# Value evictions to ScalarE with their bias as rows of the product, and row maxima placed anew

## The reference, cut to what matters

```python
x = x + attn0(layernorm(x)); x = x + experts(...); x = x + bit_mlp(...)
x = x + attn1(layernorm(x)); x = x + xattn(layernorm(x), ctx, mask); x = x + fp8_linear(...)

# each attention
q, k, v = (a @ W.T + bias for ...)          # v: 512 x 512 a sequence, bias along the features
probs = softmax(q @ k.T * 32 ** -0.5)       # for each of 16 heads (cross: clipped and masked)
out = concat_heads(probs @ v) @ Wo.T + bo
```

## Time and profile before

| | us |
|---|---|
| median of 3 runs | 1939.64 |
| lowest, highest | 1937.99, 1941.87 |
| the profiled execution | 1936.93 |
| its span | 1935.1 |
| TensorE busy | 1572.5 |
| VectorE busy | 1209.4 |
| ScalarE busy | 835.3 |
| POOL busy | 486.6 |

### The profile page before, as it was taken

The page is one execution under the profiler, slowest core; times in us unless marked ns, Lnnn a source line. Parts: engine busy times, 40 slices in busy tenths (PEclk is TensorE's granted clock), DMA queues, the critical chain, the costliest instruction groups (busy, mean ns, idle before and its releaser), DMA issues.

```text
span 1935.1 us, 28229 instructions
## 1 busy us (share of the span) xinstructions
PE 1572.5 (81%) x9252; PEld 608.8 (31%) x9253; DVE 1209.4 (62%) x1767; ACT 835.3 (43%) x991; POOL 486.6 (25%) x408
## 2 busy tenths in 40 slices
PE   2899899998948953777689999999959989989827
PEld 1323223232236631343332323233223333323213
DVE  3754747647545636999665464646544676767678
ACT  1252352533523323777635344353634445453622
POOL 1513216033120014311121212212123231414125
PEclk9999999999969986988899999999979999999968
DMA  3700202002024445100030110202222020203002
GB/s 116 238 16 22 65 0 69 18 22 65 26 105 140 138 103 114 22 1 0 11 100 10 32 34 6 60 0 65 87 72 60 22 65 22 65 1 86 0 28 87
DMA packets 80843, 106.08 MB, mean 55 GB/s; under 512 B 14112, under 2 KB 51360, under 8 KB 80672
## 3 DMA queue, kind: packets, MB, share of 16 engines
q1 hardware_dynamic: 77216, 97.14, 17.0%
q0 software_dynamic: 3584, 8.39, 2.1%
HBM read 49.26 MB, written 18.35 MB: 35 GB/s over the span
## 4 chain that ended last, share of the span: by engine, by line
PE 45%; issue 22%; DVE 18%; POOL 7%; ACT 3%; DMA 2%; DVEq 1%; POOLq 0%; ACTq 0%; SPq 0%
PE ps L398 18%; PE ps L713 13%; PE ps L799 6%; PE ps L663 3%; DVE arena L909 2%; DVE xn L186 2%; POOL arena L1117 2%; POOL arena L1177 2%; PE ps L685 1%; DVE arena L1603 1%; PE ps L1490 1%; DVE stats L175 1%; ACT arena L888 1%; DVE arena L1076 1%; POOL rstd L199 1%
## 5 line engine op out<-in xcount | busy, mean ns | idle before, releaser
L888 ACT ACTIVATE arena<-ps 128x1024 f32<-128x1024 f32 x384 | 374.0, 1023 | 346.4 <-PE ps L799 345.2
L713 PE MATMUL ps<-arena 128*32 128x512 f32 x3072 | 399.1, 625 | 33.7 <-DVE arena L943 24.4
L909 DVE TENSOR_REDUCE arena<-ps 128x2 f32<-128x1024 f32 x256 | 306.8, 1220 | 162.9 <-PE ps L663 162.9
L398 PE MATMUL ps<-xt,w 128*128 128x512 f16 (+1 forms) x1872 | 301.0, 313 | 32.4 <-DVE arena L977 20.4
L799 PE MATMUL ps<-arena 97*128 97x512 f16 (+1 forms) x768 | 221.7, 402 | 16.5 <-DVE arena L992 14.4
L398 PEld LDWEIGHTS ps<-xt,w 128*128 128x128 f16 (+1 forms) x1872 | 155.8, 101 | 169.1 <-issue 66.5
L398 PE MATMUL ps<-w,arena 128*128 128x512 f16 (+1 forms) x804 | 178.7, 379 | 12.7 <-issue 12.7
L1177 POOL TENSOR_TENSOR arena<-arena 128x512 f16<-128x512 f32 x96 | 114.9, 1199 | 239.0 <-ACT arena L877 203.4
L873 ACT ACTIVATE arena<-ps,arena 128x512 f32<-128x512 f32 x96 | 65.7, 685 | 226.0 <-PE ps L398 190.0
L1093 POOL TENSOR_TENSOR arena<-arena 128x512 f32<-128x512 f32 x36 | 50.3, 1398 | 421.7 <-DVE arena L948 421.7
L1076 DVE TENSOR_SCALAR arena<-arena 128x1024 f32<-128x1024 f32 x128 | 106.7, 839 | 65.3 <-ACT arena L888 64.8
(11 more groups left out here) (169 smaller groups left out, 1849.1 us busy)
## 6 DMA issues: line engine op xcount, KB each, us to landing
arena<-arena SPq DMA_DIRECT2D x576, 64.0 KB, 2.0
raw<-in_ctxT SPq DMA_DIRECT2D x8, 1024.0 KB, 5.4
raw<-in_ffn_parts SPq DMA_DIRECT2D x16, 512.0 KB, 3.6
sorted_x<-arena SPq DMA_DIRECT2D x1, 4864.0 KB, 27.1
arena<-sorted_x SPq DMA_DIRECT2D x19, 256.0 KB, 3.5
sorted_y<-arena SPq DMA_DIRECT2D x19, 256.0 KB, 2.1
out<-x SPq DMA_DIRECT2D x16, 256.0 KB, 2.1
x<-in_x SPq DMA_DIRECT2D x1, 3072.0 KB, 14.3
```

The source lines that it names most:

```text
L398: last = pe.matmul(out, left[l](cl[k]), right[r](cr[k]), start=start and k == 0 and a == 0, stop=stop and k == n - 1 and a == 2)
L713: last = pe.matmul(self.m.ps[HD * j:HD * (j + 1), 7 if ones else 6, :], left, self.pt[:, u % 2, j * S:(j + 1) * S], start=kb == 0, stop=kb ...
L888: act.activation(self.pt[:, u % 2, 2 * h * S:(2 * h + 2) * S], flat(self.m.ps[:, 2 * h:2 * h + 2, :]), ACT.Exp, scale=SOFTMAX_SCALE).then_ ...
L909: v.tensor_reduce(self.mx[:, g % 2, j:j + 2, t:t + 1].rearrange("p h t -> p (h t)"), self.slot_banks(item, b), AX.X, ALU.max).then_inc(sel ...
```

## The change

ScalarE evicts the four value tiles, with a copy and a scale. The bias enters through a thirteenth product in each tile, the first of its sum: `pick` (64 rows x 128, f16) has ones in rows 0 and 32 and zeros elsewhere; `vrows` holds the scaled bias in f16, its high part in rows 0 to 31 and the low rest in rows 32 to 63. Both are made once before the loop: two copies on ScalarE, one instruction on VectorE, three memsets on POOL. The bias itself is loaded into a part of the probabilities' buffer `pt` instead of one of its own, so ScalarE waits for `bias_low` before its first exponential.

In the self attentions pairs and turns get new places. In attn1 there are 11 pairs with the projections (12 before), 8 with the values (5), and 13 in the units (15); m0 goes from v0 to v1, m1 from unit 1 to v3, m2 from unit 5 to unit 6, m3 from unit 10 to unit 11. In rope there are 8 and 8 as before, and 16 in the units, of them 1, 1 and 3 in units 0, 1 and 2 (2, 1, 2); m0 goes from v0 to v2, m1 from step 0 to step 1 of unit 1, m2 from the end of unit 5 to the start of unit 6. TensorE waits with the turn of a group until the transfer of the maxima of the group before has landed.

```diff
-    WITH_PROJ = ("", "", "pp", "pp", "pp", "pp", "pp", "pp")
-    WITH_V = ("mpp", "p", "p", "p")
-    WITH_UNIT = {0: ",p,,p", 1: "m,,p,", 2: ",p,,p", 3: ",,p,", 4: ",p,,p", 5: "m,,p,", 6: ",p,,p", 7: ",,p,", 8: ",p,,p",
-                 9: ",,p,", 10: ",m,,", 13: ",,,x", 15: ",,,x"}
-    ROPE_WITH_PROJ = ("", "", "", "", "pp", "pp", "pp", "pp")
-    ROPE_WITH_V = ("mpp", "pp", "pp", "pp")
-    ROPE_WITH_UNIT = {0: ",p,,p", 1: "m,,p,", 2: ",p,,p", 3: ",,p,", 4: ",p,,p", 5: ",,p,m", 6: ",p,,p", 7: ",,p,", 8: ",p,,p",
-                      9: ",,p,", 10: ",p,,m", 13: ",,,x", 15: ",,,x"}
+    WITH_PROJ = ('', '', 'pp', 'pp', 'pp', 'p', 'pp', 'pp')
+    WITH_V = ('pp', 'mpp', 'pp', 'mpp')
+    WITH_UNIT = {1: ',p,,p', 2: ',p,,p', 3: ',,p,', 4: 'p,,,p', 5: ',p,,', 6: 'm,p,,p', 7: ',,p,', 8: ',,p,', 9: ',p,,', 11: 'm,,,', 13: ',,,x', 15: ',,,x'}
+    ROPE_WITH_PROJ = ('', '', '', '', 'pp', 'pp', 'pp', 'pp')
+    ROPE_WITH_V = ('pp', 'pp', 'mpp', 'pp')
+    ROPE_WITH_UNIT = {0: ',,p,', 1: ',m,p,', 2: 'p,,,pp', 3: ',,p,', 4: ',p,,p', 5: ',,p,', 6: 'm,p,,p', 7: ',,p,', 8: ',p,,p', 9: ',,p,', 10: ',p,,m', 13: ',,,x', 15: ',,,x'}
...
# pe_turn_max
+        if g:
+            pe.wait_ge(*self.at(self.mdma, 16 * (b * C + g)))
...
# pe, value tiles
+            pe.wait_ge(*self.at(self.pick_made, 3))
+            pe.wait_ge(*self.at(self.bias_low, 1))
             for i in range(T):
                 item = ("v", i)
                 self.wait_free(pe, item, b)
-                for c in range(C):
-                    last = three_passes(pe, self.bank(item), ..., [c], [c], start=c == 0, stop=c == C - 1)
-                    if c == C - 1:
-                        last.then_inc(self.bank_full[self.place[item][0]], 1)
+                pe.matmul(self.bank(item), self.pick[0:2 * HD, :], self.vrows[0:2 * HD, :], start=True, stop=False)
+                three_passes(pe, self.bank(item), ..., range(C), range(C),
+                             start=False).then_inc(self.bank_full[self.place[item][0]], 1)
...
+    def act_value_bias(self, act):
+        act.activation(self.vrows[0:HD, :], self.vb[0:HD, :], ACT.Copy, scale=self.vscale()).then_inc(self.bias_highs, 1)
+        act.activation(self.vhigh[HD:2 * HD, :], self.vb[HD:2 * HD, :], ACT.Copy, scale=self.vscale()).then_inc(self.bias_highs, 1)
+
+    def dve_value_bias(self, v):
+        v.wait_ge(*self.at(self.bias_highs, 2))
+        v.scalar_tensor_tensor(out=self.vrows[HD:2 * HD, :], in0=self.vb[HD:2 * HD, :], scalar=self.vscale(),
+                               in1=self.vhigh[HD:2 * HD, :], op0=ALU.mult, op1=ALU.subtract).then_inc(self.bias_low, 1)
+
+    def act_values(self, act, i, b):
+        item = ("v", i)
+        self.wait_full(act, item, b)
+        act.activation(self.v[:, i, :], self.bank(item), ACT.Copy, scale=1.0 / self.vscale()).then_inc(self.bank_free[self.place[item][0]], 1)
...
# act, in the loop, ahead of the units
+            for i in range(T):
+                self.act_values(act, i, b)
+            act.wait_ge(*self.at(self.bias_low, 1))
...
# dve, value tiles
             for i in range(T):
-                item = ("v", i)
-                self.wait_full(v, item, b)
-                v.scalar_tensor_tensor(out=self.v[:, i, :], in0=self.bank(item),
-                                       scalar=1.0 / WSCALE / (WSCALE if self.cross else 1.0),
-                                       in1=self.vb, op0=ALU.mult, op1=ALU.add).then_inc(self.bank_free[self.place[item][0]], 1)
                 self.dve_planned(v, b, "v", i)
...
# pool, ahead of its waits
+        g.memset(self.pick[0:2 * HD, :], 0.0).then_inc(self.pick_made, 1)
+        g.wait_ge(*self.at(self.pick_made, 1))
+        for k in range(2):
+            g.memset(self.pick[k * HD:k * HD + 1, :], 1.0).then_inc(self.pick_made, 1)
+        g.wait_ge(*self.at(self.pick_made, 3))
```

More of the change, by code:

```diff
@@ L436, in __init__ @@
         self.ctxn, self.sums, self.inverse = take(S), take(S), take(NQ)
-        self.vb, self.ob = take(D), take(D)
+        self.ob = take(D)
+        self.vrows, self.pick = take(D, F16), take(P, F16)
         self.pb = take(2 * C)
@@ L460, in __init__ @@
         self.pt = take(2 * HG * S).rearrange("p (n t) -> p n t", n=2)
+        self.vb, self.vhigh = self.pt[:, 1, 0:D], self.pt[:, 1, D:2 * D].bitcast(F16)[:, 0:D]
         if cross:
@@ L496, in __init__ @@
         self.normed, self.ch, self.cl = (s(n, NB * C) for n in ("ctx_normed", "ctx_high", "ctx_low"))
+        self.bias_highs, self.bias_low, self.pick_made = s("value_bias_highs", 2), s("value_bias_low", 1), s("pick_made", 3)
         self.bias_added, self.scaled = s("bias_added", NB * T), s("gamma_applied", cross * NB * T)
@@ L757, in pe @@
                 self.wait_free(pe, item, b)
-                for c in range(C):
-                    last = three_passes(pe, self.bank(item), [lambda c: a[:, 0, c, i * P:(i + 1) * P], lambda c: a[:, 1, c, i * P:(i + 1) * P]],
-                                        [lambda c: m.w[:, 2, 0, c, :], lambda c: m.w[:, 2, 1, c, :]], [c], [c], start=c == 0, stop=c == C - 1)
-                    if c == C - 1:
-                        last.then_inc(self.bank_full[self.place[item][0]], 1)
+                pe.matmul(self.bank(item), self.pick[0:2 * HD, :], self.vrows[0:2 * HD, :], start=True, stop=False)
+                three_passes(pe, self.bank(item), [lambda c: a[:, 0, c, i * P:(i + 1) * P], lambda c: a[:, 1, c, i * P:(i + 1) * P]],
+                             [lambda c: m.w[:, 2, 0, c, :], lambda c: m.w[:, 2, 1, c, :]], range(C), range(C),
+                             start=False).then_inc(self.bank_full[self.place[item][0]], 1)
                 self.pe_planned(pe, b, "v", i)
@@ L834, in dve_audio, with vscale @@
                                op0=ALU.mult, op1=ALU.subtract).then_inc(self.audio_low, 1)
+    def vscale(self):
+        return WSCALE * WSCALE if self.cross else WSCALE
+    def act_value_bias(self, act):
[9 more added lines that the diff above has]
+        act.activation(self.v[:, i, :], self.bank(item), ACT.Copy, scale=1.0 / self.vscale()).then_inc(self.bank_free[self.place[item][0]], 1)
     def act_context(self, act, g, b):
@@ L857, in act @@
         act.wait_ge(*self.at(self.consts_done, 2 + self.cross * 5))
+        self.act_value_bias(act)
         with act.Fori(0, NB) as b:
@@ L978, in dve @@
             v.wait_ge(*self.at(self.consts_done, 7))
+        self.dve_value_bias(v)
         with v.Fori(0, NB) as b:
```

## The result

The changed kernel takes 1892.64 us as a median of 4 runs (1891.43 to 1895.96), the one before 1938.82 beside it (4 runs, 1932.21 to 1941.87): a ratio of 0.9773, with an interval of 0.9747 to 0.9799. I had forecast 1910.6 and a range of 1896 to 1928.

The account below looks back on a forecast made before the run. TensorE was taken to bound the units, with waits on VectorE and a slow clock at entries into the heads. Gains of 44 (clock up) or 13 (down) became 29: 1936.93 to 1908, plus 2.7, 1910.6 us; range 1896 to 1928.

Parts of the forecast that it names:

- I take it as kept in half of them: gain 29: Entries into the heads: TensorE's clock stays up at half of them, for a total gain of 29 us.
- both ends, 44 and 13: Whole kernel: summed gain of 44 us with the clock up everywhere, 13 with it down everywhere.
- attn1, a batch, clock up: attn1 heads: earlier values, full-speed products and one pair less later gain 4.4 us a batch; 1.6 with the clock down.
- rope, a batch, up / down: Rope heads: earlier values, less a new stall in unit 2, gain 3.5 us a batch clock up, 0.7 down.
- cross, a batch, up / down: Cross entry, three batches: values start 4.1 us earlier; gain 5.0 a batch clock up, 2.2 down; batch 1 gains 0.
- bias product, each: Value steps: each added 64-row product costs 0.22 us on TensorE's path, 10.6 in all, bounds 5.8 and 12.5.
- turn of the maxima: Self attentions: TensorE transposes, VectorE copies, the next slot 0 pair waits; 1.14 us a turn in the new places.
- start, rope and attn1: Before the loops: two ScalarE copies of 0.6 us each cost 1.2 in rope and 1.2 in attn1, 0 in cross.
- rival 1: Entries into the heads: the clock stays up at every one, giving 1896 us; chance 0.2.
- Rival 2: Entries into the heads: the clock still falls at every one, giving 1927 us; chance 0.24.
- rival 3: Entries: waits stay, bound by exponentials and the slot; moved pairs only rename them; slower, 1952.6 us; chance 0.05.
- Rival 4: ScalarE in the heads: the scaled copy brings table loads of 1.28 us before exponentials, giving 1926 us; chance 0.06.

Follow-up runs that it names:

- e6: The changed kernel, unaltered, profiled once more: 1897.38 us.
- e3b: The changed kernel with the bias product 128 rows deep instead of 64: 1884.32 us, ratio 0.9723 to the kernel before.
- e10: e9 with the making of the bias rows moved ahead of the third weight matrix in rope and attn1: 1882.89 us, ratio 0.9717 to the kernel before.
- e9: The changed kernel with the 128-row bias product and, in rope alone, e7's places: 1881.96 us, ratio 0.9709 to the kernel before.
- e1: The changed kernel with pairs and maxima in their old places, keeping the ScalarE evictions and bias products: 1934.65 us, ratio 0.999 to the kernel before.
- e2: The kernel before with only the new places and the turn's added wait, VectorE still evicting with the bias: 1905.84 us, ratio 0.9835.
- e4: The changed kernel without the bias product, the values' bias left out: 1891.04 us, ratio 0.978 to the kernel before.
- e5: The kernel before, unaltered, profiled once more: 1936.96 us.
- e7: The changed kernel with m1 behind unit 1's scores, unit 0 empty and pairs respread in both self attentions: 1890.08 us, ratio 0.9762 to the kernel before.

## Why the prediction was off

The failing step is in the sum: **"I take it as kept in half of them: gain 29"**. The price of both ends, 44 and 13, was made of two parts, how often the clock falls at an entry and what a fall costs; both were set too dark, the cost above all: with the clock down rope gained 3.2 to 3.3 a batch where the sum had 0.7.

- How often. In the first profile after, it stayed up at all four attn1 entries, three of four in cross and one of four in rope: 8 of 12. In e6 it was again 8 (three, four and one).
- What it costs. "If the clock falls as before, those slow products and the slow scores (2.8 together) come back", I wrote, and by that 4.4 became 1.6 in attn1 and 3.5 became 0.7 in rope. Before, the clock was down from 1236.3 to 1243.1, 6.8 us, and for as long in rope and in attn1's batches 1 and 2 (3.4 in batch 4). After, it was down for 3.4 us in every entry that fell (also e3b: 1208.0 to 1211.5), with half the work in it, and that cost 1.5 us a batch, read from equal work: 104.89 and 103.35, both in e3b. I had priced a fall after the change like one before it. That falls at these entries are always the shorter ones is not shown: in e10's first rope batch it was 6.8 again.

Not all of the 18 us is of this step. The base has "add 2.7 at the end", the distance from the profiled execution to the median before; after, the median lies 3.3 below the profiled execution (1892.64 and 1895.96). That makes 6.0 of the 18, and no property of the change. The other 12 are the 41.0 between the profiled executions against 29: attn1's periods and heads gained 20.1 where half of each end made 12.0, rope's 13.0 for 8.4, cross's 10.5 for 10.8; the three stretches up to a first u0 cost 7.6 where I had 2.4 (they also hold the first batches' added products, which the sum counts with the batches), and the last stretch gave 5.2 by chance.

The terms, each as a gain in us:

| step | predicted | measured |
|---|---|---|
| attn1, a batch, clock up | 4.4 | 5.0 |
| rope, a batch, up / down | 3.5 / 0.7 | 5.0 / 3.2 to 3.3 |
| cross, a batch, up / down | 5.0 / 2.2 | 3.4 |
| bias product, each | -0.22 | -0.28 to -0.32, -0.43 in cross |
| turn of the maxima | -1.14 | -0.65 in attn1, -0.67 in rope |
| start, rope and attn1 | -1.2 each | -1.05, -2.1 |
| eviction on ScalarE | 0.69 | 0.60 |

*The product* was mis-sized: outside my bounds of 5.8 to 12.5, at some 16 for all 48. I had priced a 64-row product by products that stand beside others of their own shape. Here it stands alone, in cross between 128-row ones and in the self attentions between a 32-row pair and 128-row ones, and e3b shows that the 64 rows are the cost, since 128 rows take 0.22 in cross. By the rule of the Trainium skill quoted in the prediction ("TensorE: Matmul & The Clock Gate", section "Why this matters for your kernels": few rows take as long as a full product) all 48 were 10.8, an estimate; the runs have the 128-row form at or a little under that price (0.17 to 0.22) and the 64-row form above it.

*The turn* was too dear, since the first pair behind it goes into slot 1 and does not wait (1212.52, then 1212.73 in the timeline of attn1); only a pair in slot 0 does, for 0.16 to 0.50.

*Cross* gained 3.37 a batch where 5.0 stood for the clock up: 0.8 of the difference is four products at 0.43 and not 0.22, and 0.9 is the clock, given back in unit 13. "No wait before the first scores, and values 4 us earlier" came as the mechanism had it, at 3.4.

*The start.* TensorE's brackets grew by 2.0 in rope (3.14 to 5.14) and 2.1 in attn1 (4.02 to 6.11), but a longer bracket is not the cost where it also begins earlier: in rope TensorE started again only 1.05 later (55.49 for 54.44). In attn1, counted from its first projection, it did so 2.1 later (15.65 for 13.57). ScalarE's two copies were right (0.61 and 0.63 for "0.6 each"). The other 0.8 us in attn1 is ScalarE's wait for the fourth weight matrix (1.78 for 0.96), ahead of the copies. That wait differs from profile to profile; e9's bracket in rope, for the same code, is 5.78.

*Rope's new stall* in unit 2, predicted as 1.4, came as 1.33:

```profile
347.91 0.39 PE L664 MATMUL ps<-arena 32*128 32x512 f16 x2 [1.33 <-DVE arena L935]
```

*The reason* named for the self attentions was wrong in one half. I read "released by VectorE" in the brackets of the entry, and had VectorE's evictions beside it. The steps for attn1 and rope, though, are worked from slots, exponentials and the number of pairs before the values, and only rope's longer turn of m0 has an eviction in it; so the numbers held although e1 and e2 show that the evictions' move gives little there: in attn1 it saves 0.69 a batch and its four products cost 1.10, and in rope it comes out a little above its products (periods of 119.4 after, 119.7 in e2, clock down in both). Beyond its own price it pays in cross (e1: 3.2 a batch, a product of 1.7 a batch already taken off).

*The rivals.* The nearest is rival 1, the clock up everywhere, at 1896, too high by 3. That it came so near is luck: its premise did not hold (4 of 12 fell), terms too small made up for it, and its gain of 44 is above the 41.0 between the profiled executions. The Trainium skill ("TensorE: Matmul & The Clock Gate", section "HAM oscillation") puts falls down to idle gaps between bursts of products; my reading of it, that short gaps then cost nothing, would have given the better number. This reading is not borne out: in e3b's attn1 batch 3 the clock fell with an entry idle of 0.76 in all, and in the same code one batch later it did not. Rival 2 (it falls at every entry) is refuted; so is rival 3, since attn1's entry shrank by 4.4. But its premise, that the slot and not VectorE's work for the values holds the entry, is what e1 shows; what failed is its conclusion that moved pairs then give nothing (e2). Rival 4: the table loads are still four, all before attn1's batches, none in the heads. The forecast's mild losses in attn1, a slow transfer of m0 or a late m3, did not show. In rope, where I had put nothing on m0's later place, unit 0 of batch 1 waited 1.79 for a transfer (1.22 before); the later batches did not wait.

What stays open: what decides whether the clock falls at one of these entries, and why e4's median gained so little of its 15.6 us.

## What to carry to other kernels

Ask of an idle bracket which instruction of the releasing engine ended it, and what that instruction had waited for: VectorE's reduction in a slot used in turn has little to do with VectorE's load. Moving load off that engine (e1) gave nothing clear of noise, while moving pairs out of the way (e2) gave 31 us. A stall that costs 3 us by itself can cost 2 more in the slow clock behind it, so price both, and do not take the length of the slow stretch over from the kernel before (6.8 us there, 3.4 here). When a thin place is filled, the fall may come at the next one (cross unit 13). And read the cost of a wait from where the engine starts again, not from the bracket alone. A small product set between large ones is priced in its place, and may be cheaper at full height.

## What was not expected of the hardware

- One 64-row product at the head of a group of twelve 128-row ones adds 0.28 to 0.32 us in the self attentions and 0.43 in cross; with 128 rows it adds 0.17 to 0.22. The kernel gains 8 us by the taller product (1892.6 and 1884.3).
- With the same instructions the granted clock fell in one batch and not in the next: e2, e3b, e9 and e10 all alternate in attn1, with periods near 103.35 and 104.87; the changed kernel kept it in all four in one profile and lost it once in the other (e6).
- The last stretch, whose code no edit touches, took 93.4 to 93.7 us in the profiles of the changed kernel, e3b, e4, e9 and e10, and 98.8 to 99.0 in those of before, e1, e2, e5, e6 and e7; e6 is the changed kernel again. A comparison of two single profiles can carry 5 us of that.
